# The output pass of a graph transformer layer: two of seven tiles of a step go over ScalarE and GpSimd

## What is computed

```python
xn = layernorm(x)
x = x + gcn(xn, W1, b1, W2, b2, edges) + mix(xn)   # two graph convolutions; a linear-attention mixer
z = layernorm(x)
w = z @ wr + br                                    # one weight per node
sel = the KSEL nodes of the largest w              # KSEL = 6249 of 12500
y = gelu(z @ w1 + fb1) @ w2 + fb2
out = x + z + (y * w for the nodes of sel, 0 for the others)
```

## Time and profile before

| | |
|---|---|
| median of 3 runs | 5299.94 us |
| lowest and highest | 5289.96 and 5303.3 us |
| the profiled execution | 5257.22 us |
| its span | 5255.2 us |
| busy: TensorE, VectorE, ScalarE, GpSimd | 52%, 33%, 23%, 62% of the span |
| output pass, from the first line 1510 to the end | 5207.99 to 5255.2 us |

### The profile page before, as it was taken

One profiled execution on the slowest core, in us unless ns is written; L12 is line 12 of the kernel. 1 busy time (PEld: TensorE's weight loads), 2 busy tenths in 40 slices (PEclk: granted clock), 3 DMA queues, 4 the chain that ended last, 5 costly groups with the idle time before them and its releaser, 6 DMA issues.

```text
span 5255.2 us, 60640 instructions
## 1 busy us (share of the span) xinstructions
PE 2747.2 (52%) x16358; PEld 2418.8 (46%) x16359; DVE 1735.5 (33%) x4541; ACT 1210.3 (23%) x2622; POOL 3257.7 (62%) x3493
## 2 busy tenths in 40 slices
PE   6733444344334333434336666656666666665663
PEld 5633333333333333333335555555555555555552
DVE  8522223223222322322213333333333333333336
ACT  2411111111111111111003323323323332332331
POOL 3466666666666666666656666666666666666650
PEclk6766666666666666666658878888888888887886
DMA  4211111111111111111221111111111111111116
GB/s 117 64 48 48 49 49 48 48 48 48 47 48 49 48 48 49 48 47 48 52 58 49 50 47 50 49 48 49 50 49 50 49 50 49 49 50 47 50 46 199
DMA packets 191366, 288.61 MB, mean 55 GB/s; under 512 B 59596, under 2 KB 137588, under 8 KB 191094
## 3 DMA queue, kind: packets, MB, share of 16 engines
q0 software_dynamic: 106496, 218.32, 16.0%
q1 hardware_dynamic: 83572, 68.55, 4.2%
q10 hardware_dynamic: 1232, 1.05, 0.1%
HBM read 249.19 MB, written 38.49 MB: 55 GB/s over the span
## 4 chain that ended last, share of the span: by engine, by line
another core or an unknown queue 39%; PE 22%; issue 15%; DVE 9%; ACT 8%; DVEq 6%; POOL 1%; DMA 0%; ACTq 0%; SPq 0%; POOLq 0%
PE bank L880 8%; PE bank L745 5%; PE bank L865 3%; ACT arena L620 3%; ACT L609 2%; PE bank L863 2%; DVEq L331 1%; DVE acc L1189 1%; DVE arena L1256 1%; ACT gW L609 1%; DVEq L1189 1%; ACT arena L612 1%; PE bank L872 1%; DVEq L1178 1%
## 5 line engine op out<-in xcount | busy, mean ns | idle before, releaser
L492 POOL DMA_INDIRECT arena<-table,idx_now x3328 | 3149.5, 946 | 1719.2 <-issue 939.8
L745 PE MATMUL bank<-arena 128*128 128x128 f32 x6656 | 1181.7, 326 | 161.0 <-DVE arena L1178 83.9
L745 PEld LDWEIGHTS bank<-arena 128*128 128x128 f32 x6656 | 1120.0, 243 | 200.6 <-issue 95.3
L1189 DVE SCALAR_TENSOR_TENSOR acc<-bank,from_base,acc 128x128 f32 x416 | 145.7, 350 | 2937.4 <-remote 2523.0
L781 PE MATMUL bank<-ident,arena 128*128 128x128 f32 x196 | 67.2, 446 | 1104.0 <-ACT arena L590 1104.0
L1178 DVE SCALAR_TENSOR_TENSOR arena<-dst_of,base_col,bank 128x1024 f32 (+1 forms) x416 | 532.4, 1280 | 97.4 <-DVE acc L1189 71.2
L781 PEld LDWEIGHTS bank<-ident,arena 128*128 128x128 f32 x196 | 28.3, 203 | 1123.3 <-ACT arena L590 1123.2
L889 PE MATMUL bank<-arena 128*128 128x256 f32 x1568 | 395.6, 397 | 164.5 <-ACT arena L620 164.2
L880 PE MATMUL bank<-arena 128*128 128x128 f32 x3136 | 405.5, 284 | 73.1 <-ACT arena L616 54.7
L880 PEld LDWEIGHTS bank<-arena 128*128 128x128 f32 x3136 | 378.4, 197 | 91.9 <-ACT arena L616 69.4
L889 PEld LDWEIGHTS bank<-arena 128*128 128x128 f32 x1568 | 291.8, 196 | 215.7 <-ACT arena L620 181.4
(11 more groups left out here) (245 smaller groups left out, 3068.0 us busy)
## 6 DMA issues: line engine op xcount, KB each, us to landing
arena<-table,idx_now POOLq DMA_INDIRECT x3328
base_rows<-arena SPq DMA_DIRECT2D x98, 128.0 KB
xs<-in_x_dram SPq DMA_DIRECT2D x6, 1792.0 KB, 16.4
acc<-base_rows SPq DMA_DIRECT2D x9, 896.0 KB, 10.1
out_dram<-acc SPq DMA_DIRECT2D x8, 896.0 KB, 8.1
table<-acc SPq DMA_DIRECT2D x7, 896.0 KB, 4.7
table<-acc SPq DMA_DIRECT2D x98, 64.0 KB
arena<-base_rows SPq DMA_DIRECT2D x5, 896.0 KB, 11.8
```

What stands on the lines that cost most here:

```text
L492: pool.indirect_dma_start(ring[:, quarter * HALF + k, :], None, table[layer], bass.IndirectOffsetOnAxis(ap=idx_now[:, gg % 2, c:c + 1], ax ...
L745: last = nc.tensor.matmul(visit_sum[h][:, 0:F], S[:, h, k, :], ring[:, quarter * HALF + k, :], start=(k == 0), stop=(k == HALF - 1))
L1189: last = dve.scalar_tensor_tensor(a, visit_sum[h][:, 0:F], mask[:, ds(turn, 1)], a, ALU.mult, ALU.add)
```

## The change

`ON_DVE = HG - 2` = 5. VectorE handles tiles 0 to 4 of each step as before and signals `s_tf` after the fifth. As soon as `selw` is made it signals `s_sel`. ScalarE then multiplies tiles 5 and 6 of each step in `xs`, in place, by their column of `selw`, and signals `s_wsel` once a step. GpSimd waits for that and for the slot, adds the two tiles of `xs` to the two of the slot with one instruction of 128x512, and signals `s_tg`. SP waits for both `s_tf` and `s_tg` ahead of each store. Slots, loads, stores and their order stay.

```diff
@@ -193,6 +193,7 @@
         SLOTS = acc_slots + arena_slots
+        ON_DVE = HG - 2
@@ -307,7 +308,10 @@
+        s_sel = sem("selection_weights_ready")
+        s_wsel = sem("rows_of_gpsimd_weighted")
         s_tf = sem("tail_rows_ready")
+        s_tg = sem("tail_rows_of_gpsimd_ready")
@@ -419,6 +423,7 @@
             for j in range(STEPS):
                 sp.wait_ge(s_tf, j + 1)
+                sp.wait_ge(s_tg, j + 1)
                 if j < STEPS - 1:
@@ -504,6 +509,13 @@
             gather_layer(1)
 
+            for i in range(STEPS):
+                pool.wait_ge(s_wsel, i + 1)
+                pool.wait_ge(s_tl[i % SLOTS], 16 * (i // SLOTS + 1))
+                t = i * HG
+                pool.tensor_tensor(slots[i % SLOTS][:, ON_DVE:HG, :], slots[i % SLOTS][:, ON_DVE:HG, :],
+                                   xs[:, t + ON_DVE:t + HG, :], ALU.add).then_inc(s_tg, 1)
@@ -620,6 +632,12 @@
+            act.wait_ge(s_sel, 1)
+            for i in range(STEPS):
+                for t in range(i * HG + ON_DVE, (i + 1) * HG):
+                    last = act.activation(xs[:, t, :], xs[:, t, :], ACT.Copy, scale=selw[:, t:t + 1])
+                last.then_inc(s_wsel, 1)
@@ -1503,9 +1521,10 @@
             link(dve.tensor_tensor(selw, selw, gt, ALU.add))
+            dve.sem_inc(s_sel, 1)
             for i in range(STEPS):
                 dve.wait_ge(s_tl[i % SLOTS], 16 * (i // SLOTS + 1))
-                for j in range(HG):
+                for j in range(ON_DVE):
                     t = i * HG + j
                     last = dve.scalar_tensor_tensor(slots[i % SLOTS][:, j, :], xs[:, t, :], selw[:, t:t + 1],
                                                     slots[i % SLOTS][:, j, :], ALU.mult, ALU.add)
```

## The result

The changed kernel takes 5311.0 us in the median of 19 runs (5303.13 to 5318.48), the kernel before 5299.56 us (19 runs, 5289.96 to 5307.42). The ratio is 1.0022, with a 95% interval of 1.0014 to 1.0027: some 7 to 14 us slower. That is small, but it is measured, and it has the sign that was forecast. The executions differ by tens of us ahead of the pass (its first product-and-add came at 5207.99 us in the profiled run of before, at 5253.31 in that of the changed kernel and at 5208.89 in a second profile of it), so the whole spans of single profiles are not compared here, only the pass: from the first product-and-add to the end of the span. It took 47.2 us before and takes 56.8 now (5310.1 - 5253.31), 9.6 us more.

A forecast was written before the change was run, and what follows sets the result against it. The pass was taken as bound by when the first store goes and whether a next one follows. Two stores out by 17.8 us, then 12.82 MB at 384 GB/s, gave about 8 us more: 5299.94 + 8 = 5308, range 5293 to 5323.

The forecast's parts named there:

- That the transfers, and not VectorE's sum, set the pass: Output pass: bound by when the first store goes and whether a next one follows; 14.65 MB take 38.2 to 40.4 us.
- The detail on the tail: Last 12 us of the pass before: transfers at 330 GB/s follow VectorE's pace, 0.917 MB each 2.79 us, 329 GB/s.
- The hold: Output pass: each GpSimd addition of 128x512 blocks VectorE for 0.41 + 0.57 = 0.98 us, bounds 0 and 1.3.
- The round: Output pass: one VectorE instruction plus one GpSimd block of it, 0.398 + 0.98 = 1.38 us.
- The order of turns: Output pass: engines alternate, GpSimd runs ahead; VectorE's first three steps end at 4.0, 10.9 and 17.8 us; chance 0.45.
- The end: End of the span after the last store: 5261.8 to 5264.0, 6.6 to 8.8 us later, 8 taken.
- late starvation: Output pass, from about the sixth GpSimd addition: no turns until VectorE stops, +9 to +12 us; chance 0.2 with a kept port.
- a kept port: Output pass: GpSimd holds VectorE through twelve additions, first store at 15.8 us, +11, 5311; chance 0.2 with late starvation.
- Full starvation from the start: Output pass: GpSimd adds only after VectorE's first 60 instructions, first store at 25.1 us, +20.5, 5320; chance 0.15.
- no conflict: Output pass: VectorE and GpSimd don't block each other, first store at about 2.6 us, 1.6 to 3.8 earlier, 5297; chance 0.15.

The follow-up runs named there:

- the run without a conflict: Changed kernel, but VectorE's product-and-add takes its third operand from a PSUM bank instead of the slot; pass 46.4 us, whole-time ratio 0.9997.
- The probes: Changed kernel with steps made to wait for GpSimd, varying its addition's arrival, releaser or VectorE's unbroken run; additions took 1.26 to 1.58 us or, starved, 2.95 and more.
- the two probes: Changed kernel with 16 extra product-and-adds a step (256 or 64 columns), GpSimd released one later each step; additions starved from 2.64 and 3.01 us into VectorE's run.

## Why the prediction was right, point by point

**That the transfers, and not VectorE's sum, set the pass.** Right, and the strongest reading of the profile: VectorE ended 1.0 us later than before, the pass 9.6 us later, and with 5.6 us less on VectorE (one tile over TensorE) the pass didn't get shorter. The room is small, though: with GpSimd paced the early stores came sooner, and there VectorE's held instructions did set the pass. The detail on the tail was wrong: 330 GB/s were taken for VectorE's pace because 329 is what one store each 2.79 us gives. Ten microseconds of the tail run at 345 GB/s before as in the run without the addition, so VectorE had no part in it. So the room for any gain was 1.0 us, not 1.6 to 3.8, and the forecast of the end was too kind by the same error: the last 12 us of the changed kernel ran at 351 GB/s, not at 384, which is 1.1 us.

**ScalarE.** Taken 0.5 us an instruction; its 28 took 493 to 510 ns and one each 0.40 (11.31 us together), with no table load. GpSimd's first addition began 0.94 us into the pass, not 1.3.

**GpSimd.** Taken 1.14 us alone; the 14th, which nothing held, took 1256 ns, as in the run without a conflict (1255 to 1267).

**The hold.** Taken 0.98 us, from 0.41 for 256 columns and 0.57 for 256 more; measured 1.00 (and 0.47 for 256 columns). The round was taken at 1.38 us and was 1.40. This was the term that decides, and it came from a few rows of a stage 5000 us earlier, which shared only the kind of operands. The sharp check is the run with a bank for the third operand: with one SBUF input on VectorE the hold is gone.

**The order of turns.** First store 4.0 forecast, 4.1 measured; second 10.9 and 11.2; third 17.8 and 18.2. After that the forecast says 1.99 us a step and two more holds, VectorE through at 41.7; it was through at 39.9, since the 13th and 14th additions held nothing: they came after it.

**The end.** The pass was to end 6.6 to 8.8 us later than before, and 8 were taken. It ended 9.6 us later in the profile and 11.4 in the medians, whose interval of 7 to 14 us holds both. The rest up to 9.6 is the third store, 0.4 us later than forecast, and the slower tail, 1.1. A small misreading lies beside it: the last bytes land 0.8 us before the end of the span in both kernels (before, nothing moves after 5254.5), not 1.5. The size alone doesn't show the mechanism, since the forecast had late starvation at +9 to +12 and a kept port at +11; the third store and the rounds of 1.40 us do.

**The rivals.** Full starvation from the start, no conflict and a kept port didn't happen. Late starvation did, and it was there in the rows of before (8.92 us at 56.38), but it was priced for the sixth addition. It struck the 13th, when the transfers were so far behind that nobody waited for it: the store of step 12 was issued at 43.5 us into the pass, 2.5 us after that addition was through. The prediction gave no condition for it. The probes show that it isn't chance, and give part of the condition.

## What to carry to other kernels

Look for what an engine's work feeds before pricing what it saves: here more than a quarter of VectorE's pass could go for a gain of 1 us, because the stores behind it were the limit, and the delay of the first stores cost about 6.4 us. A helper that must do one piece a step, and is let run ahead, takes its turns from the steps that are due first; pacing it gave back 6.4 of 9.6 us here. And work given from VectorE to GpSimd, both reading SBUF with VectorE reading two operands there, costs VectorE more than doing it (0.54 us of hold against 0.40 of work for each 128x256).

## What the runs showed of the hardware

GpSimd and VectorE took turns one by one with both queues full, twelve times in a row and within 27 ns of each other (1436 to 1463), in both profiles of the changed kernel. Their exclusion is what the Trainium skill states in "SBUF — State Buffer", section "Who interferes with whom": one input of VectorE from PSUM instead of SBUF and it was gone (475 to 481 ns for each of 70 instructions). By that section of the Trainium skill the one that comes second is blocked until the other's instruction has finished. The runs show more than that. In the two probes, an addition that arrived when VectorE had been running two-input instructions unbroken, from a pause on, for 2.6 us or more (256 columns) or 3.0 (64 columns) lost at every one of the following boundaries until VectorE paused. Behind a turn of GpSimd, turns were still given after up to 4.0 us, so this is no general limit. The longest waits were 33 instructions and 14.3 us in the changed kernel, 45 and 18.5 us with one tile shared. While it lasts, the held one is GpSimd, and VectorE's instructions take their free 471 to 475 ns.

A 128x512 addition on GpSimd took 1.26 us with nothing in its way. From the 4497 ns that the Trainium skill gives for 2048 columns in "GPSIMD Engine Reference", section 3.1, an estimate would be 1.12; the runs here show 1.26.

Stores to HBM ran at 385 GB/s for 18 us on one core, and at 346 to 351 in their last 12 us, with issued stores still to move in both. A store with nothing else moving ran at 346 too (5259.3 to 5260.3 in the changed kernel); why the middle is faster stays open. The 358 GB/s of the Trainium skill's page "DMA: Bandwidth & Descriptors", which the prediction weighed, is by its section "Measured" what each of two cores on one memory gets when both stream; here only one core ran, and 358 was no limit.
